# Attention loop of a Trainium2 kernel in units of two heads: fp32 scores in row groups, value products two key blocks behind, group ends moved with a 16-column reciprocal

## What is computed

```python
x = x + attention(layernorm(x))          # first part
x = x + moe(layernorm(x))                # second part, with a shared expert

def attention(x):
    q, k, v = split(x @ w_qkv)           # 16 heads of 32
    q, k = rope(q), rope(k)
    q = layernorm(q) * ln_scale + ln_bias    # per head, over 32
    k = layernorm(k) * ln_scale + ln_bias
    a = tril((q @ k.T) ** 4)             # fourth power, causal
    out = (a / a.sum(-1, keepdims=True)) @ v
    return out @ w_out
```

## Time and profile before

| | us |
|---|---|
| median of 3 runs | 1253.88 |
| lowest and highest | 1252.7, 1258.45 |
| span of the profiled execution | 1278.8 |
| PE busy | 1013.0 (79%) |
| DVE busy | 782.5 (61%) |
| ACT busy | 571.1 (45%) |
| POOL busy | 503.3 (39%) |
| mean granted PE clock | 0.883 |

### The profile page before, as it was taken

How to read it: one execution, slowest core, us unless ns; L and a number is a source line. 1 busy time by engine, 2 the same in 40 slices (tenths; PEclk the granted TensorE clock), 3 DMA queues, 4 the chain that set the end, 5 groups by cost and what they waited for, 6 DMA issues and landing times. The chain is left out here.

```text
span 1278.8 us, 21813 instructions
## 1 busy us (share of the span) xinstructions
PE 1013.0 (79%) x5786; PEld 483.4 (38%) x5787; DVE 782.5 (61%) x1641; ACT 571.1 (45%) x1018; POOL 503.3 (39%) x738
## 2 busy tenths in 40 slices
PE   5956799666997669976588889888888888878893
PEld 2422245222444214442145445344344344434341
DVE  2855578587695885858955866444544545544442
ACT  2377624767147672366735324333333333323330
POOL 0047500556003751026631102555555555555552
PEclk9977898677996689967787889999999999989997
DMA  8015430144501438104445786777877778877774
GB/s 323 1 50 188 159 131 1 50 149 146 183 3 49 140 107 327 69 0 148 148 149 178 264 321 216 188 171 178 187 185 179 170 177 191 192 154 183 169 178 77
DMA packets 76782, 194.36 MB, mean 152 GB/s; under 512 B 9920, under 2 KB 11072, under 8 KB 75328
## 3 DMA queue, kind: packets, MB, share of 16 engines
q1 hardware_dynamic: 58816, 150.58, 34.5%
q0 software_dynamic: 17920, 43.26, 18.9%
HBM read 132.72 MB, written 61.10 MB: 152 GB/s over the span
## 5 line engine op out<-in xcount | busy, mean ns | idle before, releaser
L606 PE MATMUL bank<-arena,xgT 128*128 (+1 forms) x1152 | 287.4, 387 | 4.0 <-ACT xgT L817 3.1
L853 POOL TENSOR_TENSOR s_p<-s_p,c_causal 128x128 f32<-128x128 f32 x256 | 128.8, 530 | 400.0 <-DVE s_p L1193 397.6
L552 PE MATMUL bank<-s_p,vtok 128*32 128x128 f32 (+3 forms) x512 | 118.0, 605 | 95.9 <-DVE arena L1143 49.5
L810 ACT ACTIVATE hT<-bank 128x512 f16<-128x512 f16 x96 | 57.3, 597 | 276.5 <-PE bank L616 264.6
L462 PE MATMUL bank<-arena 128*128 128x512 f32 x384 | 168.6, 597 | 2.0 <-issue 2.0
L606 PEld LDWEIGHTS bank<-arena,xgT 128*128 128x128 f16 x1152 | 109.6, 100 | 133.5 <-issue 44.4
L627 PE MATMUL bank<-wd,hT 128*128 128x512 f16 x576 | 152.7, 405 | 0.7 <-ACT hT L810 0.7
L898 POOL DMA_INDIRECT out<-yy,sidx x80 | 128.4, 1605 | 45.7 <-issue 44.7
L861 POOL TENSOR_TENSOR arena<-arena 128x768 f16<-128x768 f32 x68 | 115.7, 1702 | 71.9 <-ACT arena L684 71.5
L817 ACT ACTIVATE xgT<-bank 128x1024 f16<-128x1024 f16 x96 | 98.2, 1023 | 90.7 <-PE bank L597 89.1
L1367 DVE TENSOR_SCALAR yy<-bank,hsc 128x512 f32<-128x512 f32 x80 | 60.0, 750 | 125.8 <-DMA out<-yy,sidx 106.6
(11 more groups left out here) (155 smaller groups left out, 1453.3 us busy)
## 6 DMA issues: line engine op xcount, KB each, us to landing
wd<-w_scratch SPq DMA_DIRECT2D x82, 512.0 KB
arena<-w_experts SPq DMA_DIRECT2D x34, 768.0 KB, 5.9
w_scratch<-arena SPq DMA_DIRECT2D x34, 768.0 KB, 4.5
arena<-w_scratch SPq DMA_DIRECT2D x17, 1024.0 KB, 8.0
xin<-x SPq DMA_DIRECT2D x5, 1024.0 KB, 9.1
arena<-x SPq DMA_DIRECT2D x4, 1024.0 KB, 7.1
x_scratch<-arena SPq DMA_DIRECT2D x4, 1024.0 KB, 4.5
xn_scratch<-vtok SPq DMA_DIRECT2D x4, 1024.0 KB, 5.0
```

What stands on the lines that cost most here:

```text
L552: mm = pe.matmul(bank[6 + n][r, P * kb:N], w, s_p4[:, (i - 1) % 2, j, 0:N - P * kb], start=(kb == 0), stop=(kb == MB - 1), skip_group_chec ...
L606: mm = pe.matmul(bank[2 + k][:], xgT[:, k, xh * EC + c, :], w, start=(c == 0 and xh + wh == 0), stop=(c == EC - 1 and xh == 1))
L853: pool.tensor_tensor(d, d, C["causal"][:], ALU.mult).then_inc(p4_masked, 1)
```

## The change

The loop now works in units of two heads (unit u = 2 i, 2 i + 1; UNITS = 32 per block):

- `q16`, `k16`, `qk32` and the factor QS are gone. ACT writes one fp32 copy per operand to `qT` and `kT`; `split_qk` is gone.
- Scores: one fp32 product per head, in row groups, instead of three fp16 ones. Semaphores count units.
- ACT squares two heads (two banks) in one instruction; ACT's `fourth` is gone.
- DVE makes the fourth power of all four heads, two heads per instruction.
- POOL masks two heads (256 columns) per instruction.
- Value products come two iterations behind the scores (LAG = 2), so PE's loop has 18 rounds.
- `finish` transposes bank 7 in 32x32 blocks, takes the reciprocal of one column per block (16 columns; the 32 columns of a block are alike), transposes it back with a broadcast, and multiplies. It stands behind the powers of i = 5, 9 and 13, and once behind the loop.

The routing, the weight pieces and the transfers keep their places.

```diff
@@ TensorE, the loop
-                for i in range(NG * MB + 1):
-                    if i < NG * MB:
+                for i in range(UNITS // 2 + LAG):
+                    if i < UNITS // 2:
                         g, kb = divmod(i, MB)
...
+                        for u in (2 * i, 2 * i + 1):
+                            if u >= 2:
+                                pe.wait_ge(sq_done, b * UNITS + (u - 1))
...
+                            for j in (u % 2 * 2, u % 2 * 2 + 1):
+                                r = slice(D * j, D * j + D)
+                                mm = pe.matmul(bank[j][:, 0:N - P * kb], kT[r, g, P * kb:P * kb + P],
+                                               qT[r, g, P * kb:N], start=True, stop=True)
+                            mm.then_inc(scores_ps, 1)
-                    if i:
-                        g, kb = divmod(i - 1, MB)
+                    if i >= LAG:
+                        g, kb = divmod(i - LAG, MB)
                         if kb == 0 and g:
                             pe.wait_ge(att_done, b * NG + g)
@@ ScalarE, qkT
-                    act.activation(dst[:, 0, :, m * P:m * P + P], quad(bank[6 + w]), ACT.Identity,
-                                   bias=ln_b[:, 0:1], scale=ln_s[:, 0:1])
-                    if m or not isinstance(b, int):
-                        act.wait_ge(qk_lo, b * (2 * MB) + (2 * m + w - 1))
-                    act.activation(qk32[:, w, :].rearrange("p (c n) -> p c n", c=4), quad(bank[6 + w]), ACT.Identity,
+                    act.activation(dst[:, :, m * P:m * P + P], quad(bank[6 + w]), ACT.Identity,
                                    bias=ln_b[:, 0:1], scale=ln_s[:, 0:1]).then_inc(qkT_sb, 1)
@@ ScalarE, the loop
+                    for u in (2 * i, 2 * i + 1):
+                        j = u % 2 * 2
+                        act.wait_ge(scores_ps, b * UNITS + (u + 1))
+                        if u >= 2:
+                            act.wait_ge(p4_done, b * UNITS + (u - 1))
+                        act.activation(s_sq[:, j:j + 2, 0:w], wide(j)[:, :, 0:w], ACT.Square).then_inc(sq_done, 1)
@@ GpSimd
+                        d = s_p4[:, i % 2, j:j + 2, 0:P]
+                        pool.tensor_tensor(d, d, C["causal"][:].unsqueeze(1).to_broadcast([P, 2, P]),
+                                           ALU.mult).then_inc(p4_masked, 1)
@@ VectorE, finish
                 dve.wait_ge(pv_done, b * (NG * MB) + (g * MB + MB))
-                dve.reciprocal(rec, bank[7][:])
+                blocks = lambda a: a.rearrange("p (c i) -> p c i", i=D)
+                dve.transpose(den_t, bank[7][:])
+                dve.drain()
+                dve.reciprocal(inv[:], blocks(den_t)[:, :, 0])
+                dve.drain()
+                dve.transpose(blocks(rec), inv[:].unsqueeze(2).to_broadcast([P, N // D, D]))
                 dve.drain()
                 dve.tensor_tensor(attT[:, g, :], bank[6][:], rec, ALU.mult).then_inc(att_done, 1)
@@ VectorE, the loop
+                    for u in (2 * i, 2 * i + 1):
+                        j = u % 2 * 2
+                        dve.wait_ge(sq_done, b * UNITS + (u + 1))
+                        s2 = s_sq[:, j:j + 2, 0:N - P * kb]
+                        dve.tensor_tensor(s_p4[:, i % 2, j:j + 2, 0:N - P * kb], s2, s2, ALU.mult).then_inc(p4_done, 1)
-                    if i and kb == 0:
+                    if i > MB and kb == 1:
                         finish(b, i // MB - 1)
```

More of the change, by code:

```diff
@@ L53 @@
 XS, WS = 1024.0, 256.0
-QS = 64.0
 HMAX = 4096.0
@@ L61 @@
 CH = NCOL // P
+UNITS = NG * MB * 2
+LAG = 2
 NEG = 1.0e30
@@ L161, in build @@
         xnT = over([EC, N])
-        q16, k16 = (over([NG, N]).bitcast(F16).rearrange("p g (h n) -> p h g n", h=2) for _ in range(2))
+        qT, kT = (over([NG, N]) for _ in range(2))
         s_sq = over([HG, N])
@@ L234, in build @@
         moe.close()
-        bank = [ctx.enter_context(nc.psum_tensor(f"bank{i}", [P, 512], F32)) for i in range(8)]
+        scores = ctx.enter_context(nc.psum_tensor("scores", [P, HG, 512], F32))
+        bank = [scores[:, j, :] for j in range(HG)] + [
+            ctx.enter_context(nc.psum_tensor(f"bank{i}", [P, 512], F32))[:] for i in range(HG, 8)]
         quad = lambda bk: bk[:].rearrange("p (c n) -> p c n", c=4)
+        wide = lambda j: scores[:, j:j + 2, :]
         oct16 = lambda bk: bk[:].bitcast(F16).rearrange("p (c n) -> p c n", c=8)
@@ L523, in sequence @@
                 qk_transposes(b, MB - 1)
-                pe.wait_ge(qk_lo, b * (2 * MB) + 2 * MB)
+                pe.wait_ge(qkT_sb, b * (2 * MB) + 2 * MB)
                 pe.wait_ge(v_sb, b * MB + MB)
-                for i in range(NG * MB + 1):
-                    if i < NG * MB:
+                for i in range(UNITS // 2 + LAG):
+                    if i < UNITS // 2:
                         g, kb = divmod(i, MB)
[L531 to L535, removed]
-                                pe.wait_ge(logits_sb, b)
[L537 to L541, removed]
-                    if i:
-                        g, kb = divmod(i - 1, MB)
+                        for u in (2 * i, 2 * i + 1):
+                            if u >= 2:
+                                pe.wait_ge(sq_done, b * UNITS + (u - 1))
+                            if u == 1 and before is not None:
+                                pe.wait_ge(logits_sb, b)
+                            for j in (u % 2 * 2, u % 2 * 2 + 1):
[5 more added lines that the diff above has]
+                        g, kb = divmod(i - LAG, MB)
                         if kb == 0 and g:
@@ L754, in sequence @@
                     copy_logits(before)
[L756 to L760 removed]
+                for i in range(UNITS // 2):
                     w = N - P * (i % MB)
[L762 to L774 removed]
+                    for u in (2 * i, 2 * i + 1):
[4 more added lines that the diff above has]
+                        act.activation(s_sq[:, j:j + 2, 0:w], wide(j)[:, :, 0:w], ACT.Square).then_inc(sq_done, 1)
                     if i == 0 and before is not None:
```

64 lines of the change are left out of this document (16 added, 48 removed).

## The result

The changed kernel takes 1288.4 us in the median (1286.1 to 1292.8), the kernel before 1256.2 on the same chip: a ratio of 1.0256, 95% interval 1.0217 to 1.0294. It is 32 us **slower**. The prediction was 1250 us, range 1222 to 1275. It was wrong in sign and size.

A forecast was written before the change was run, and what follows sets the result against it. DVE and POOL excluding each other was taken to bound the first loop, DVE itself the later three. Starts -7.6, first loop +0.5, later loops +3 gave -4 us from the 1253.9 median: 1250 us, range 1222 to 1275.

The forecast's parts named there:

- Ahead of the loops: Before each loop, one copy per operand lets scores start 1.9 us sooner, four times: -7.6 us.
- Durations: Instruction times in the loops: squares 22.7 us and powers 26.4 us a loop, group end 2.5 us, mask 0.69 us.
- the exclusion: In the loops, two-operand SBUF instructions of DVE and POOL exclude each other: 4.67 us per first-loop iteration against 4.44.
- The moved end: Group ends at i = 5, 9, 13: following product covered except at i = 13 of later loops, 2.7 us idle there.
- routing work ... covers the product: Later loops, i = 5 and 9: about 4 us of DVE routing work covers the product's 1.8 to 3.6 us.
- POOL's backlog of masks and subtraction: First loop: about 3 us of POOL work covers the end and most of the product, shrinking PE's 13.2 us waits.
- the move of the end does nothing: Rival at group ends: the wait merely shifts an iteration, 3 us a loop at i = 13, about 1258 us; chance 0.07.
- The sum for a later loop: Later loops: DVE 75.3 us busy plus 16.4 idle, 91.7 against 90.4; taken as +1 us, three times.
- Waits of PE are the bound: Rival in the loops: PE's group-end waits set the time, each loop loses 8 to 13 us, 1194 to 1214; chance 0.22.
- The exclusion is what counts: Rival in later loops: powers lose 10.6 us to POOL instead of 3.0, total 1273 us; chance 0.20.
- Row groups do not overlap: Rival for fp32 scores: row groups run serially, a pair takes 3.4 us cold, total 1265 to 1290; chance 0.06.
- over 95 (exclusion): Sign of being wrong: later loops over 95 us, read as DVE and POOL blocking each other.

The follow-up runs named there:

- e2: The changed kernel with the old group end, one 512-column reciprocal; ratio to the kernel before 1.0494, loops 401.8 us.
- e3: The kernel before with the new short group end alone (transposes, 16-column reciprocal); ratio to the kernel before 0.9933, loops 332.5 us.
- e4: The kernel before with the fp32 scores alone, no split of q and k; ratio to the kernel before 1.0090, loops 348.2 us.
- e5: e1 with the second unit's fourth power on ACT, so powers are shared; ratio to the kernel before 0.9966, loops 328.8 us.
- e1: The changed kernel with value products one behind and group ends back at i = 4, 8, 12; ratio to the kernel before 1.0105, loops 363.5 us.
- e7: The changed kernel with group ends back at i = 4, 8, 12, products still two behind; ratio to the kernel before 1.0023, loops 356.8 us.
- e8: The changed kernel with POOL's subtraction cut to 8 of 768 columns (low halves wrong); ratio to the kernel before 0.9903, loops 340.1 us.

## Why the prediction was wrong, point by point

The loops' 37.9 us, each part by the runs that differ in it alone (the parts depend on the order in which they are put together; e2 and e3 show by how much, and the third row takes in all that the first two do together):

| part | from | us, four loops | predicted |
|---|---|---|---|
| fp32 scores | before to e4 | +5.2 | 0 |
| short end | before to e3 | -10.5 | -4.6 in each later loop |
| two heads wide, powers shared | e3, e4 to e5 | -8.9 | not named |
| all powers on DVE | e5 to e1 | +34.7 (some 3.5 of it clock) | +10.7 of DVE a loop, mostly given back |
| two behind | e1 to e7 | -6.7 (some 3.5 of it clock) | not named |
| end moved | e7 to after | +24.1 | +2.7 in each later loop |

The change came out 36 us above the forecast (+32 against -4). By the traces 16 of them are the moved end (24.1 against three times 2.7) and 18 the rest of the loops (before to e7 +13.8 where the sums without the move's 2.7 give -4.6).

**Ahead of the loops: right.** -8.9 measured (0.6, 3.4, 2.0 and 2.9, not 1.9 each), -7.6 predicted; the scores start 0.87 us after PE's last work instead of 2.75.

**Durations: right.** Squares 21.8 us a loop (22.7 predicted), powers in a later loop 29.7 (26.4 + 4), the end 2.6 (2.5), the mask 0.72 clean (0.69). In the mean the mask takes 1.05 us, and 1.05 also in e8's second loop, without the subtraction: it is the powers that hold it up. I had charged the exclusion to DVE alone. One reading was wrong: ACT's 66.4 us of the first loop before are a sum of groups that overlap; the stretch has it busy 62.9.

**The moved end: the step that failed.** The prediction let no product show behind the ends at i = 5 and 9 ("routing work ... covers the product") and 2.7 us at i = 13. The second loop shows 1.63, 1.12 and 3.85 us of DVE waiting there: the routing work at i = 5 ends 1.6 us too early. In the first loop I let "POOL's backlog of masks and subtraction" cover the end and most of the product. A backlog on POOL delays the masks; it gives DVE nothing to do, and DVE waited 15.1 us. That is why the first loop lost 4.9 us instead of 0.5, and e7's first loop, without the move, is at 71.8, 2.4 under the kernel before. I looked for what covers the product and did not ask whether it had to be behind the end at all. The rival "the move of the end does nothing" had the mechanism (the wait only shifts), priced at 3 us a loop for i = 13 alone; the runs give 5.4 to 7.3.

**The sum for a later loop: mis-sized on both sides.** Busy DVE 75.3 predicted, 77.5 measured; idle 16.4 predicted, 22.9 measured. e7's second loop has 16.2 us idle and 78.6 busy, 94.8 us. That this meets the 16.4 is luck. Item by item the second loop has 3.2 us ahead of the first power (3.1 predicted), 2.4 behind the sigmoid (2.7), 1.1 at the counting products (2.5), 6.6 behind the moved ends (2.7), 3.3 at the norm (3.4) and 6.3 in short gaps ("about 2 in drains"). e7 has no wait behind its ends, 0.8 at the counting products and 6.5 in short gaps. So the term that the runs show wrong besides the moved end is the short gaps, some 4 us a loop, and the busy sum is 3.3 short. This left e7 4.4 to 6.4 us a later loop above the kernel before. For ACT's relief I booked nothing, and no run separates it from DVE's load: together the move of ACT's powers to DVE costs 34.7 / 4 = 8.7 us a loop, close to the 10.7 of DVE alone. I weighed that load against gains (the end, idle time) that do not depend on where the powers are. The right comparison is e5, the kernel of e1 with the powers shared: 5.1 us shorter in the first loop and 8.1, 12.3 and 9.2 in the later ones.

**The rivals.** "Waits of PE are the bound" had PE's 13 us in hand: e7 removes them and the first loop gains 2.4 us, not 8 to 13. ACT then waits 9.5 us of that loop for the weights, and in the later loops DVE's load fills the place. "The exclusion is what counts" predicted the sign and 1273 us; the dearer subtraction is 10 us of the loss, not 23. Its floor of 78 us for the first loop does not hold either: e7 does the same powers, masks and subtractions in 71.8. "Row groups do not overlap" is refuted by the 2.09 us. Of the signs, "over 95 (exclusion)" came, but mostly for another cause, the moved end.

**The granted clock, in no term of the sum.** The four loops ran at 0.80, 0.74, 0.75 and 0.74 before, at 0.71, 0.67, 0.67 and 0.66 after, and at 0.78, 0.65, 0.64 and 0.65 in e7. e7 is some 5 us a later loop shorter than after at no higher a clock, so the moved end's cost is not the clock's. What the lower clock costs either of them against the kernel before, no run separates.

## What to carry to other kernels

Where a wait between two engines is to be relaxed by going one step further behind, move one side only; if the producer moves with the consumer, the distance is what it was, and with as many buffers as steps the next producer waits too. Before work is joined on one engine, add up that engine in the stage where it is fullest: from e5 to e1 the second loop has 11 us less on ACT, which had slack, and 14 more on DVE, and the four loops are 35 us longer. And when a program's instructions change in number, look at the first instruction behind each jump before a time is put down to the edit.

## What the runs showed of the hardware

- A reciprocal of 128x512 out of PSUM takes 3.35 us, of 128x16 in SBUF 0.254; a 128x512 fp32 transpose in blocks takes 0.71. Two transposes and the short reciprocal, 1.9 us with the drains between them and behind them, do the work of the 3.35.
- Four heads' fp32 scores in four row groups take 2.09 us at a granted clock of 0.50, eight passes of 512 columns in all, about the same as the value products in column groups (1.94).
- Behind the jump back in a loop DVE stood for 1.0 to 1.1 us in most kernels, 1.6 and 3.0 in e3, and 6.9 to 8.6 in e2, e4 and e5, by the place of the loop in its program; idle instructions ahead of the loop brought e5's back to 1.0.
- POOL's 768-column subtraction costs the kernel before 30.5 us and the changed one 40.8, though POOL is never full. The Trainium skill (SBUF — State Buffer, Who interferes with whom) calls the ports that the two engines share an exclusive lock; the masks' mean of 1051 ns against 717 clean shows that POOL is held up as DVE is. That the other engine is fully blocked for a whole instruction stands there for DVE's two-port modes, and the 71.8 us of e7's first loop are below what it would give.
